# One one-hot matrix a batch instead of three, with shifted copies of keys and values: a two-layer cross-attention kernel

## The chip, the cores and the metric

The kernel runs on one core of one Trainium2 chip. The metric is the device time of one execution in microseconds (us). In the profile PE is the matrix engine (PEld its weight loads), DVE the vector engine, ACT the scalar engine, POOL the GpSimd engine, and SP the engine whose queue issues most of the DMA transfers.

## The reference, cut to what matters

There are 16 batches of 512 tokens by 256 features, and a context of 64 positions by 256 features for each batch. Two attention layers follow each other. The first has 16 heads of 16 features, and a token sees only the three context positions around its index:

```python
q = split(rmsnorm(x_tokens, gamma_q) @ Wq.T)      # 512 queries a batch, 16 heads of 16
k = split(kn @ Wk.T); v = split(kn @ Wv.T)        # 64 keys and values a batch
mask = abs(ctx_pos - ctx_index_per_token) <= 1    # positions index-1, index, index+1
w = where(mask, square(relu(q @ k.T / sqrt(hd))), 0)
out = (w / max(w.sum(-1), EPS_DEN)) @ v
x = x_tokens + out @ Wo.T
```

The second layer is a plain softmax attention over the 64 context positions with GELU on queries, keys and values, followed by a projection, a residual and a LayerNorm. Everything is float32; the kernel splits the operands of the large products into a high and a low part.

## The kernel before, in words

**Tiling.** A batch is one unit of work: 512 tokens by 256 features, held as two feature groups of 128 partitions. Keys and values of the first layer are computed once, at the start, for all batches, and stored in `kv0` as 128 rows: rows 0 to 63 hold the high parts of the 64 positions, rows 64 to 127 the low parts. Column group 0 is keys, column group 1 values.

**Picking by one-hot.** Instead of scoring all 64 positions, the kernel picks the three keys and the three values of each token by a matrix product with a one-hot matrix. For each shift `s` (0, 1, 2) DVE builds a 128x512 matrix that is 1 where the row's position, moved by `s - 1`, equals the token's index (`build_onehot`, L684). PE multiplies `kv0` by it: `picked_keys` (L386) gives keys 512 tokens wide, two products a shift; `picked_values` (L392) gives values 256 features wide, four products a shift. DVE multiplies picked keys with the queries (L697) and picked values with the normalised weights (`attend`, L738), and PE transposes and sums the results (`turn`, L411).

**Stages.** The 16 batches run as a software pipeline: step i handles the first half of layer one of batch i (`f`), the second half of batch i-1 (`b`), and the end of batch i-2 (`n`). Each engine has its own list of instructions, written by hand; an engine works strictly in the order of its list and waits at semaphores. At the end of step i, PE already picks the first keys of batch i+1 (`first_keys`).

**The start.** Before step 0 PE computes the keys and values of the context, eight tiles of two products (L324). ACT and DVE round and split them (L553, L670). SP moves them into `kv0` by 16 DMAs (L243, L244), eight for batches 0 to 7 and eight for batches 8 to 15; each group of eight waits for DVE (`prep_dve`). PE waits for the first eight of them (`kv0_in[0]`) before `first_keys(0)`. Behind the 16, SP's list has the loads of tokens and indices of batches 2 and 3 (L211, L212), the move of the second layer's values into `vfd` (L255), and then in each step the load for the batch three ahead.

**POOL** computes the low part of the tokens (L283), the reciprocal square roots, and the last scale and shift with the store of the output.

Of the kernel before, what the change touches and what calls it, by code (L numbers as in the profile page):

```python
# [19 lines left out]
C_ID, C_SEL, C_POS, C_EPS, C_END = 0, 128, 224, 227, 228  # L20


def xattn_pair(nc: bass.Bass, xT, ctx, ctxT, idx, vectors, wq0T, wk0T, wv0T, wo0T,
# [9 lines left out]
    with es:  # L33
# [10 lines left out]
        pos = [cst[:, C_POS + s:C_POS + s + 1] for s in range(SHIFTS)]  # L44
# [18 lines left out]
        onehot = sb("onehot", [P, SHIFTS, T], f32r)  # L63
# [4 lines left out]
        att = qkp[:, SHIFTS:2 * SHIFTS, :].rearrange("p s (j d) -> p s j d", j=TT)  # L68
# [4 lines left out]
        wn = sb("wn", [P, SHIFTS, TT, H])  # L73
# [16 lines left out]
        bufs = sb("bufs", [P, 8, DC * T])  # L90

        xsq, q0, xpT, q1T = (bufs[:, n, :].rearrange("p (c t) -> p c t", c=DC) for n in (0, 3, 4, 5))

        zn, zo = (bufs[:, n, :].rearrange("p (j d) -> p j d", j=TT) for n in (6, 7))
# [11 lines left out]
        v1T = bufs[:, 4:6, :]  # L106
        ctxT_sb = bufs[:, 6:8, :]
        vfn = rows(bufs[:, 6:8, :])
# [17 lines left out]
        kv0_in = [sem(f"kv0_in_{t}") for t in range(2)]  # L126
        prep_mm, prep_act, prep_dve, kvh_cp, vf_mm, vf_copied, vfd_in = map(sem, (
# [77 lines left out]
        def _(sp):  # L205
# [47 lines left out]
            for half in range(2):  # L253
                for odd in range(2):
                    sp.dma_start(vfd[half * K:(half + 1) * K, odd::2, :], vfn[odd * K:(odd + 1) * K, :, :]).then_inc(vfd_in, 16)  # L255
            for read in range(1, B - RING + 1):
# [5 lines left out]
                load(read + (RING - 1))  # L262
            for h in range(2):
# [50 lines left out]
        def _(pe):  # L314
# [68 lines left out]
            def picked_keys(f, s, bank0):  # L383

                for g in range(DC):
                    i = mm(ps[:, bank0 + g, :], kv0[:, f, 0, g * P:(g + 1) * P].bitcast(f32r), onehot[:, s, :], start=True, stop=True)  # L386
                i.then_inc(kg_mm, 1)

            def picked_values(f, s, bank0):

                for j in range(TT):
                    i = mm(ps[:, bank0 + j // 2, (j % 2) * D:(j % 2 + 1) * D], onehot[:, s, j * P:(j + 1) * P],  # L392
# [13 lines left out]
            def turn(f, s):  # L406

                pe.wait_ge(att_ready, 3 * f + s + 1)
                for g in range(DC):
                    for j in range(TT):  # L410
                        i = mm(ps[:, g, j * P:(j + 1) * P], att[:, s, j, g * P:(g + 1) * P], ident,  # L411
                               is_transpose=True, start=(s == 0 and j == 0), stop=(s == SHIFTS - 1), skip_group_check=True)
                    if s == SHIFTS - 1:
# [11 lines left out]
            def step(f, b, n, last=False):  # L425
# [62 lines left out]
                if f is not None:  # L488
# [5 lines left out]
                    picked_values(f, 0, 6)  # L494
# [154 lines left out]
        def _(dve):  # L649
# [28 lines left out]
            def build_onehot(f, shifts):  # L678
# [6 lines left out]
                if s == SHIFTS - 1:  # L685
                    i.then_inc(onehot_ready, 1)
# [162 lines left out]
```

## Time and profile before

| | |
|---|---|
| median of 3 runs | 422.99 us (420.45 to 423.73) |
| profiled execution, its own time | 423.02 us |
| its span in the trace | 421.2 us |
| PE busy | 384.7 us, 91% |
| DVE busy | 300.5 us, 71% |
| ACT busy | 222.4 us, 53% |
| POOL busy | 143.7 us, 34% |
| DMA engines, q1 (SP's queue) | 24.11 MB, 20.0% of 16 engines' span |

A share of busy time is an average over the whole span. The page also cuts the span into 40 slices and gives the busy share of each; the first four to six slices, the start, look different from the rest, which repeats with the period of a step. The time that lies outside the span is 423.02 less 421.2, which is 1.8 us. A time in the text is counted from the span's start.

### The profile page before, as it was taken

The numbers are of one execution on the slowest core, as the hardware profiler recorded it, in microseconds if no ns is written. First come the engines' busy times: TensorE is split into PE (matmuls) and PEld (weight loads), VectorE is DVE, ScalarE is ACT, GpSimd is POOL, SyncE is SP. The second block draws the span as 40 slices with busy tenths as digits, with TensorE's granted clock in tenths as the row PEclk, the third lists the DMA queues.
The fourth block names the chain that finished last, engine by engine and source line by source line (L and its number), as shares of the span: only waits on it lengthen the run. The fifth ranks groups of instructions, "written<-read, shape, count | busy, mean of one in ns | idle before, by whom it ended". The sixth has DMA issues, their size and how long they took to land.

```text
span 421.2 us, 5934 instructions
## 1 busy us (share of the span) xinstructions
PE 384.7 (91%) x2256; PEld 285.3 (68%) x2256; DVE 300.5 (71%) x592; ACT 222.4 (53%) x369; POOL 143.7 (34%) x100
## 2 busy tenths in 40 slices
PE   4799798999999999999999999999999999998770
PEld 1258666686868686868686868686868777776550
DVE  0334459587979797878787887878787879697614
ACT  0754412356556564646464656565656474737441
POOL 0102202023535353535353535353535353415151
PEclk9999999999999999999999999999999999999985
DMA  8901985802121212121212112020202101010111
GB/s 238 321 38 43 219 213 158 193 2 75 51 75 52 75 51 75 51 75 51 75 53 72 54 55 71 30 95 15 93 26 82 42 0 52 0 51 0 50 51 50
DMA packets 20333, 32.35 MB, mean 77 GB/s; under 512 B 1489, under 2 KB 11729, under 8 KB 20305
## 3 DMA queue, kind: packets, MB, share of 16 engines
q1 hardware_dynamic: 18144, 24.11, 20.0%
q0 software_dynamic: 2160, 7.87, 5.3%
q8 instruction: 18, 0.29, 0.3%
q14 instruction: 11, 0.08, 0.1%
HBM read 17.29 MB, written 8.39 MB: 61 GB/s over the span
## 4 chain that ended last, share of the span: by engine, by line
PE 78%; ACT 6%; issue 4%; DVE 4%; DMA 3%; SPq 2%; POOL 2%; ACTq 0%; DVEq 0%; POOLq 0%
PE ps L373 11%; PE ps L375 10%; PE ps L374 10%; PE ps L411 9%; PE ps L509 7%; PE ps L465 7%; PE ps L386 7%; PE ps L392 5%; PE ps L441 4%; PE ps L324 4%; PE ps L516 3%; ACT bufs L629 2%; DMA cst<-consts 2%; PE ps L478 2%; DMA kv<-qkp 1%
## 5 line engine op out<-in xcount | busy, mean ns | idle before, releaser
L283 POOL TENSOR_TENSOR x_lo<-x_ring,x_hi 128x1024 fp32r<-128x1024 f32 x16 | 38.1, 2380 | 124.9 <-ACT x_hi L568 124.9
L585 ACT ACTIVATE bufs<-ps,nbias,rstd 128x256 f32<-128x256 f32 x64 | 32.4, 563 | 65.5 <-issue 55.5
L303 POOL TENSOR_TENSOR bufs<-bufs,lng_row 128x1024 f32<-128x1024 f32 x15 | 35.9, 2394 | 84.5 <-ACT bufs L585 84.5
L738 DVE TENSOR_TENSOR qkp<-ps,wn 128x1024 f32<-128x1024 f32 x48 | 57.3, 1221 | 5.9 <-PE ps L392 4.5
L697 DVE TENSOR_TENSOR qkp<-ps,bufs 128x1024 f32<-128x1024 f32 x48 | 57.1, 1218 | 5.2 <-PE ps L386 5.2
L411 PE MATMUL ps<-cst,qkp 128*128 128x128 f32 x384 | 44.8, 273 | 0.0
L411 PEld LDWEIGHTS ps<-cst,qkp 128*128 128x128 f32 x384 | 42.6, 143 | 0.1
L386 PE MATMUL ps<-onehot,kv 128*128 128x512 f32 x96 | 34.4, 440 | 4.7 <-DMA kv<-qkp 2.1
L509 PE MATMUL ps<-k1T,bufs 128*128 128x64 f32 x256 | 32.0, 278 | 5.4 <-ACT bufs L629 5.4
L305 POOL TENSOR_TENSOR bufs<-bufs,lnb_row 128x1024 f32<-128x1024 f32 x15 | 35.5, 2366 | 1.2
L509 PEld LDWEIGHTS ps<-k1T,bufs 128*128 128x128 f32 x256 | 29.8, 191 | 8.9 <-ACT bufs L629 8.9
L392 PEld LDWEIGHTS ps<-kv,onehot 128*128 128x128 f32 x192 | 27.1, 189 | 10.0 <-ACT bufs L585 5.3
L392 PE MATMUL ps<-kv,onehot 128*128 128x256 f32 x192 | 33.3, 299 | 0.3 <-DVE wn L760 0.2
L465 PE MATMUL ps<-qkp,cst 128*32 128x512 f32 x192 | 30.7, 598 | 0.5 <-DVE qkp L697 0.5
L465 PE MATMUL ps<-bufs,cst 128*32 128x512 f32 x64 | 30.5, 598 | 0.0
L751 DVE TENSOR_REDUCE den<-ps 128x64 f32<-128x192 f32 x16 | 5.7, 358 | 34.3 <-ACT ps L620 34.3
L294 POOL TENSOR_TENSOR rstd<-var,minus_half 128x4 f32<-128x4 f32 x16 | 16.5, 1031 | 38.3 <-DVE var L720 38.3
L373 PE MATMUL ps<-xp_hi,wh_q 128*128 128x512 f32 x64 | 26.5, 414 | 2.3 <-DVE xp_lo L732 2.3
L732 DVE TENSOR_TENSOR xp_lo<-bufs,xp_hi 128x512 fp32r<-128x512 f32 x32 | 20.8, 688 | 10.3 <-ACT xp_hi L601 10.1
L640 ACT ACTIVATE o_hi<-ps 128x512 fp32r<-128x512 f32 x32 | 17.4, 595 | 19.9 <-PE ps L411 19.9
L373 PE MATMUL ps<-x_hi,wh_q 128*128 128x512 f32 x64 | 27.0, 422 | 0.0
L629 ACT ACTIVATE bufs<-ps,vec 128x512 f32<-128x512 f32 x32 | 22.0, 688 | 9.3 <-PE ps L375 9.1
(96 smaller groups left out, 820.8 us busy)
## 6 DMA issues: line engine op xcount, KB each, us to landing
x_ring<-xT SPq DMA_DIRECT2D x16, 512.0 KB, 3.6
out<-bufs POOLq DMA_DIRECT2D x15, 512.0 KB, 3.4
idx_ring<-idx SPq DMA_DIRECT2D x16, 256.0 KB, 4.2
kv<-qkp SPq DMA_DIRECT2D x8, 256.0 KB, 4.9
vfd<-bufs SPq DMA_DIRECT2D x4, 512.0 KB, 7.9
bufs<-ctxT SPq DMA_DIRECT2D x2, 512.0 KB, 6.5
qkp<-ctx SPq DMA_DIRECT2D x1, 1024.0 KB, 7.3
kv<-xp_hi SPq DMA_DIRECT2D x2, 256.0 KB, 4.1
```

Of the source, the lines that this page charges most:

```text
L283: G.tensor_tensor(x_lo[:, :, :], x_ring[:, f % RING, :, :], f32_view(x_hi[:, :, :]), ALU.subtract).then_inc(xl_ready, 2)
L303: G.tensor_tensor(zo, zn, lng_row[:, :].unsqueeze(1).broadcast_to([P, TT, D]), ALU.mult).then_inc(zg_ready, 1)
L373: mm(o, hi, m_hi, start=start, stop=False)
L374: mm(o, lo, m_hi, start=False, stop=False)
L375: last = mm(o, hi, m_lo, start=False, stop=stop)
L386: i = mm(ps[:, bank0 + g, :], kv0[:, f, 0, g * P:(g + 1) * P].bitcast(f32r), onehot[:, s, :], start=True, stop=True)
L392: i = mm(ps[:, bank0 + j // 2, (j % 2) * D:(j % 2 + 1) * D], onehot[:, s, j * P:(j + 1) * P], kv0[:, f, 1, :].bitcast(f32r), start=True, s ...
L411: i = mm(ps[:, g, j * P:(j + 1) * P], att[:, s, j, g * P:(g + 1) * P], ident, is_transpose=True, start=(s == 0 and j == 0), stop=(s == SHI ...
L465: i = mm(ps[32 * s:32 * s + 32, 4, :], sum_sel[:, g if s < SHIFTS else 2, :], qk[:, s, g, :] if s < SHIFTS else xsq[:, g, :], start=(g == ...
L509: i = mm(ps[:, 3, j * K:(j + 1) * K], q1T[:, c, j * P:(j + 1) * P], k1T[:, c, bass.ds(b * K, K)], start=(c == 0), stop=(c == DC - 1))
L697: V.tensor_tensor(qk[:, s, :, :], ps[:, bank0:bank0 + 2, :], q0, ALU.mult).then_inc(qk_ready, 1)
L738: V.tensor_tensor(att[:, s, :, :].rearrange("p j (h d) -> p (j h) d", d=HD), ps[:, bank0:bank0 + 2, :].rearrange("p a (h d) -> p (a h) d", ...
```

## The change

**One one-hot matrix.** A batch has a single one-hot matrix now, for the token's own position; the shifts 0 and 2 of the mask are no longer matrices. There are two buffers of it, used in turn, so that the matrix of the next batch is built while the present one is read.

**Shifted copies.** For the neighbours the keys and values themselves are moved: `kvs` holds, for each of two buffers, a copy of the batch's rows moved one row up (for index+1) and one moved one row down (for index-1). The copies are DMAs from `kv0`, issued by SP, four a batch, each 63 rows of 2 KB; the rows that no copy fills are zero from a memset of POOL at the start (`kvs_zero`). `first_keys` waits for the copies of its batch (`kvs_in`). The copies of batches 0 and 1 stand in SP's list behind the 16 DMAs into `kv0`; those of batch i+1 stand in step i behind the loads of tokens and indices.

**Order of the picks.** Keys are picked in the order index+1, index-1, centre. Values of both neighbours are picked in one product 512 wide for each of the four token tiles (`picked_neighbours`, two products a call, two calls), and the centre in four products 256 wide (`picked_centre`). `attend` has three calls of 1024 elements a partition as before, the layouts of `att` and `wn` are reordered to match, and `turn` has 8 transposes a call as before.

```diff
-        pos = [cst[:, C_POS + s:C_POS + s + 1] for s in range(SHIFTS)]
+        pos = cst[:, C_POS:C_POS + 1]
-        onehot = sb("onehot", [P, SHIFTS, T], f32r)
+        onehot = sb("onehot", [P, 2, T], f32r)
-        wn = sb("wn", [P, SHIFTS, TT, H])
+        wn = sb("wn", [P, TT, SHIFTS, H])
+        kvs_all = sb("kvs", [P, 2, 2, 2, D])
...
         @block.sync
+            def shifted(i):
+                r = i % 2
+                for lo in (0, K):
+                    sp.dma_start(kvs[lo:lo + K - 1, r, 0, :, :], kv0[lo + 1:lo + K, i, :, :]).then_inc(kvs_in[r], 16)
+                    sp.dma_start(kvs[lo + 1:lo + K, r, 1, :, :], kv0[lo:lo + K - 1, i, :, :]).then_inc(kvs_in[r], 16)
+            sp.wait_ge(kvs_zero, 1)
+            sp.wait_ge(kv0_in[0], 16 * 8)
+            shifted(0)
+            shifted(1)
             for i in range(2, RING):
...
+            def next_shifted(i):
+                if i == 8:
+                    sp.wait_ge(kv0_in[1], 16 * 8)
+                sp.wait_ge(kvs_in[i % 2], 64 * (i // 2))
+                sp.wait_ge(vg_mm, 3 * (i - 1))
+                shifted(i)
             for read in range(1, B - RING + 1):
...
                 load(read + (RING - 1))
+                next_shifted(read + 1)
+            for i in range(B - RING + 2, B):
+                next_shifted(i)
...
         @block.gpsimd
+            G.memset(kvs, 0.0).then_inc(kvs_zero, 1)
...
         @block.tensor
             def first_keys(f):
                 pe.wait_ge(onehot_ready, f + 1)
+                pe.wait_ge(kvs_in[f % 2], 64 * (f // 2 + 1))
                 picked_keys(f, 0, 4)
+            def picked_neighbours(f, pair, bank0):
+                for a in range(2):
+                    j = 2 * pair + a
+                    i = mm(ps[:, bank0 + a, :], onehot[:, f % 2, j * P:(j + 1) * P],
+                           kvs[:, f % 2, :, 1, :].bitcast(f32r),
+                           start=True, stop=True)
+                i.then_inc(vg_mm, 1)
...
-                    picked_values(f, 0, 6)
+                    picked_neighbours(f, 0, 6)
                     pe.wait_ge(wn_ready, f + 1)
-                    picked_values(f, 1, 4)
+                    picked_neighbours(f, 1, 4)
-                    picked_values(f, 2, 6)
+                    picked_centre(f, 6)
...
         @block.vector
+            def build_onehot(f):
                 dve.wait_ge(idx_in, 16 * f + 16)
-                if not first(f):
-                    dve.wait_ge(vg_mm, 3 * f)
-                for s in shifts:
-                    i = V.tensor_scalar(onehot[:, s, :], idx_ring[:, f % RING, :], pos[s], None, ALU.is_equal)
+                if f > 1:
+                    dve.wait_ge(vg_mm, 3 * (f - 1))
+                V.tensor_scalar(onehot[:, f % 2, :], idx_ring[:, f % RING, :], pos, None, ALU.is_equal).then_inc(onehot_ready, 1)
...
                 if f is not None:
+                    if not last:
+                        build_onehot(f + 1)
                     dve.wait_ge(w_ready, f + 1)
...
-                    if not last:
-                        build_onehot(f + 1, range(0, 2))
...
-                if f is not None and not last:
-                    build_onehot(f + 1, range(2, SHIFTS))
```

**SP at the start, before.** These are the rows of SP's list from the last two DMAs into `kv0` on (`kv`), with the loads of batches 2 and 3 behind them.

```order
L243 DMA kv<-o_lo 64x4x256
L244 DMA kv<-qkp 64x4x256
L211 DMA x_ring<-xT 128x2x512 [waits idx_in,x_in]
L212 DMA idx_ring<-idx 128x512
L211 DMA x_ring<-xT 128x2x512 [waits idx_in,x_in]
```

**SP at the start, in the change.** The same place, where `kvs` is the tensor of the shifted copies.

```order
L248 DMA kv<-o_lo 64x4x256
L249 DMA kv<-qkp 64x4x256
L254 DMA kvs<-kv 63x512 [waits kv0_in_0,kvs_zero]
L255 DMA kvs<-kv 63x512
L254 DMA kvs<-kv 63x512
L255 DMA kvs<-kv 63x512
L254 DMA kvs<-kv 63x512
L255 DMA kvs<-kv 63x512
L254 DMA kvs<-kv 63x512
L255 DMA kvs<-kv 63x512
L216 DMA x_ring<-xT 128x2x512 [waits idx_in,x_in]
L217 DMA idx_ring<-idx 128x512
```

Eight copies, four for batch 0 and four for batch 1, stand behind all 16 DMAs into `kv0` and ahead of the loads.

**DVE in step 1, before.** These are DVE's rows from the end of `head` to the low part of the layer's output; L684 builds a one-hot matrix.

```order
L732 TENSOR_TENSOR xp_lo<-bufs,xp_hi 128x512 [waits xph_ready] x2
L751 TENSOR_REDUCE den<-ps 128x64 [waits w_ready]
L754 TENSOR_TENSOR dcl<-den,ps 128x64 [waits den_ready]
L758 RECIPROCAL rden<-dcl 128x64 [waits dcl_ready]
L760 TENSOR_TENSOR wn<-ps,rden 128x192 [waits rden_ready]
L738 TENSOR_TENSOR qkp<-ps,wn 128x1024 [waits vg_mm,o_mm,wn_ready]
L738 TENSOR_TENSOR qkp<-ps,wn 128x1024 [waits vg_mm] x2
L684 TENSOR_SCALAR onehot<-idx_ring,cst 128x512 [waits vg_mm,idx_in]
L684 TENSOR_SCALAR onehot<-idx_ring,cst 128x512
L779 TENSOR_REDUCE smax<-ps 128x4 [waits sc_mm]
L781 TENSOR_TENSOR sdiff<-ps,smax 128x256 [waits smax_ready]
L684 TENSOR_SCALAR onehot<-idx_ring,cst 128x512 [waits vg_mm,idx_in]
```

**DVE in step 1, in the change.** The same place.

```order
L772 TENSOR_TENSOR xp_lo<-bufs,xp_hi 128x512 [waits xph_ready] x2
L726 TENSOR_SCALAR onehot<-idx_ring,cst 128x512 [waits vg_mm,idx_in]
L800 TENSOR_REDUCE den<-ps 128x64 [waits w_ready]
L803 TENSOR_TENSOR dcl<-den,ps 128x64 [waits den_ready]
L807 RECIPROCAL rden<-dcl 128x64 [waits dcl_ready]
L809 TENSOR_TENSOR wn<-ps,rden 128x192 [waits rden_ready]
L785 TENSOR_TENSOR qkp<-ps,wn 128x2x512 [waits vg_mm,o_mm,wn_ready]
L785 TENSOR_TENSOR qkp<-ps,wn 128x2x512 [waits vg_mm]
L785 TENSOR_TENSOR qkp<-ps,wn 128x4x256 [waits vg_mm]
L826 TENSOR_REDUCE smax<-ps 128x4 [waits sc_mm]
```

One build is left, and it stands ahead of the reduction of the weights (`den`) instead of behind the multiplications with the values.

**PE in step 1, in the change.** These rows take the place of L392 x4, L392 (waits wn_ready), L392 x3, the six products of the second layer's queries, and L392 x4.

```order
L422 MATMUL ps<-kvs,onehot 128x512 x2
L422 MATMUL ps<-kvs,onehot 128x512 [waits wn_ready]
L422 MATMUL ps<-kvs,onehot 128x512
L401 MATMUL ps<-xp_hi,wh_q 128x512
L402 MATMUL ps<-xp_hi,wl_q 128x512
L403 MATMUL ps<-xp_lo,wh_q 128x512
L401 MATMUL ps<-xp_hi,wh_q 128x512
L402 MATMUL ps<-xp_hi,wl_q 128x512
L403 MATMUL ps<-xp_lo,wh_q 128x512
L430 MATMUL ps<-kv,onehot 128x256 [waits att_ready]
```

Eight products 256 wide became four 512 wide; their waits stand where they stood.

## Rows read from the trace of the kernel before

**Rows 1.** The page: PE's busy tenths in 40 slices; the chain that ended last.

```profile
PE   4799798999999999999999999999999999998770
...
PE 78%; ACT 6%; issue 4%; DVE 4%; DMA 3%; SPq 2%; POOL 2%; ACTq 0%; DVEq 0%; POOLq 0%
```

**Rows 2.** Busy time by stretch (start:end, length, each engine), one whole step.

```profile
core 0: us, PE busy (x) PEld busy (x) DVE busy (x) ACT busy (x) POOL busy (x), PEclk, DMA share, GB/s
199.00:220.65 21.65, 21.28 (x134) 16.07 (x134) 17.58 (x35) 12.69 (x20) 9.20 (x6) 1.00 0.18 62
```

**Rows 3.** Timeline of SP (start, us to issue, line), DMAs into kv0 and the loads behind.

```profile
55.41 1.16 SPq L244 DMA_DIRECT2D kv<-qkp  x1
56.66 1.69 SPq L211 DMA_DIRECT2D x_ring<-xT  x1
```

**Rows 4.** Timeline of PE at the start of step 0 (idle before in brackets).

```profile
47.14 1.89 PE L367 MATMUL ps<-vfd,bufs 128*128 128x256 f32 x8
51.16 1.20 PE L386 MATMUL ps<-onehot,kv 128*128 128x512 f32 x4 [2.14 <-DMA kv<-qkp]
```

**Rows 5.** DMAs issued between 38 and 62 us: mean rate, and us to landing.

```profile
DMA packets 4680, 4.84 MB, mean 202 GB/s; under 512 B 273, under 2 KB 4369, under 8 KB 4679
...
kv<-qkp SPq DMA_DIRECT2D x8, 256.0 KB, 4.9
...
x_ring<-xT SPq DMA_DIRECT2D x1, 512.0 KB, 5.6
```

**Rows 6.** The page: DMA issues of the whole span, KB each, us to landing.

```profile
x_ring<-xT SPq DMA_DIRECT2D x16, 512.0 KB, 3.6
```

**Rows 7.** PE's first matmuls, groups of 5.9-11.5 us and 12.2-16 us (mean ns).

```profile
L324 PE MATMUL ps<-bufs,vfd 128*128 128x512 f32 x7 | 6.3, 1079 | 6.0 <-DMA bufs<-ctxT 6.0
L324 PE MATMUL ps<-bufs,vfd 128*128 128x512 f32 x10 | 4.9, 642 | 0.0
```

**Rows 8.** A stretch as in rows 2, after a wait of PE (PEclk: granted clock).

```profile
18.70:22.40 3.70, 3.70 (x5) 1.62 (x6) 2.85 (x10) 1.77 (x4) 0.00 (x0) 0.54 0.83 221
```

**Rows 9.** Waits by engine: us in total, times, longest.

```profile
POOL cmean L276 <- ACT x_ring L549: 15.8, 1, 15.8
...
PE ps L324 <- ACT k1T L553: 2.5, 1, 2.5
```

**Rows 10.** Timeline of DVE at the end of step 0.

```profile
67.75 1.27 DVE L684 TENSOR_SCALAR onehot<-idx_ring,cst 128x512 fp32r<-128x512 int32 x3
68.94 1.28 DVE L794 TENSOR_TENSOR o_lo<-ps,o_hi 128x512 fp32r<-128x512 f32 x2
```

**Rows 11.** Timeline of PE in a later step, around the picks of values.

```profile
211.09 0.40 PE L375 MATMUL ps<-xp_lo,wh_q 128*128 128x512 f32 x1
211.42 1.44 PE L392 MATMUL ps<-kv,onehot 128*128 128x256 f32 x8
212.70 0.40 PE L373 MATMUL ps<-xp_hi,wh_q 128*128 128x512 f32 x1
...
213.86 0.39 PE L375 MATMUL ps<-xp_lo,wh_q 128*128 128x512 f32 x1
214.09 0.63 PE L392 MATMUL ps<-kv,onehot 128*128 128x256 f32 x4
215.03 0.32 PE L509 MATMUL ps<-k1T,bufs 128*128 128x64 f32 x1 [0.31 <-ACT bufs L629]
```

**Rows 12.** Timeline of DVE in the same step.

```profile
210.47 0.36 DVE L751 TENSOR_REDUCE den<-ps 128x64 f32<-128x192 f32 x1 [2.00 <-ACT ps L620]
...
215.90 1.07 DVE L684 TENSOR_SCALAR onehot<-idx_ring,cst 128x512 fp32r<-128x512 int32 x2
217.06 0.42 DVE L779 TENSOR_REDUCE smax<-ps 128x4 f32<-128x256 f32 x1
```

**Rows 13.** Timeline of SP in the same step.

```profile
206.48 0.38 SPq L211 DMA_DIRECT2D x_ring<-xT  x1
```

**Rows 14.** Timeline of PE at the end of that step.

```profile
220.50 1.48 PE L386 MATMUL ps<-onehot,kv 128*128 128x512 f32 x4
```

More of the change, by code:

```diff
@@ L89, in xattn_pair @@
         nbias = sb("nbias", [P, TT])
-        bufs = sb("bufs", [P, 8, DC * T])
-        xsq, q0, xpT, q1T = (bufs[:, n, :].rearrange("p (c t) -> p c t", c=DC) for n in (0, 3, 4, 5))
-        zn, zo = (bufs[:, n, :].rearrange("p (j d) -> p j d", j=TT) for n in (6, 7))
+        kvs_all = sb("kvs", [P, 2, 2, 2, D])
+        kvs = kvs_all[:, :, :, :, :]
+        bufs = sb("bufs", [P, 7, DC * T])
+        xsq, q0, xpT, q1T = (bufs[:, n, :].rearrange("p (c t) -> p c t", c=DC) for n in (0, 2, 3, 4))
+        zn, zo = (bufs[:, n, :].rearrange("p (j d) -> p j d", j=TT) for n in (5, 6))
         def rows(t):
@@ L105, in xattn_pair @@
         kv_lo = [[rows(qkp[:, n:n + 1, :]) for n in pair] for pair in ((0, 4), (1, 5))]
[L106 to L108 removed]
+        v1T = bufs[:, 3:5, :]
+        ctxT_sb = bufs[:, 5:7, :]
+        vfn = rows(bufs[:, 5:7, :])
         raw = {n: vfd[:, 2 * i:2 * i + 2, :] for i, n in enumerate(("k0", "v0", "k1", "v1", "f1", "q0", "o0", "q1"))}
@@ L126, in xattn_pair @@
         kv0_in = [sem(f"kv0_in_{t}") for t in range(2)]
+        kvs_zero = sem("kvs_zero")
+        kvs_in = [sem(f"kvs_in_{r}") for r in range(2)]
         prep_mm, prep_act, prep_dve, kvh_cp, vf_mm, vf_copied, vfd_in = map(sem, (
@@ L385, in picked_keys, with picked_centre @@
                 for g in range(DC):
-                    i = mm(ps[:, bank0 + g, :], kv0[:, f, 0, g * P:(g + 1) * P].bitcast(f32r), onehot[:, s, :], start=True, stop=True)
+                    keys = kv0[:, f, 0, :] if s == CENTRE else kvs[:, f % 2, s, 0, :]
+                    i = mm(ps[:, bank0 + g, :], keys[:, g * P:(g + 1) * P].bitcast(f32r), onehot[:, f % 2, :], start=True, stop=True)
                 i.then_inc(kg_mm, 1)
-            def picked_values(f, s, bank0):
+            def picked_neighbours(f, pair, bank0):
[5 more added lines that the diff above has]
+                i.then_inc(vg_mm, 1)
+            def picked_centre(f, bank0):
                 for j in range(TT):
-                    i = mm(ps[:, bank0 + j // 2, (j % 2) * D:(j % 2 + 1) * D], onehot[:, s, j * P:(j + 1) * P],
+                    i = mm(ps[:, bank0 + j // 2, (j % 2) * D:(j % 2 + 1) * D], onehot[:, f % 2, j * P:(j + 1) * P],
                            kv0[:, f, 1, :].bitcast(f32r),
@@ L404, in queries0, with turn @@
                     product(ps[:, e, :], *weight("q0", c, e), x_hi[:, c, :], x_lo[:, c, :], c == 0, c == DC - 1, q0_mm)
-            def turn(f, s):
-                pe.wait_ge(att_ready, 3 * f + s + 1)
+            def turn(f, part):
+                pe.wait_ge(att_ready, 3 * f + part + 1)
+                if part < CENTRE:
+                    tiles = [(2 * part + a, s) for a in range(2) for s in range(2)]
+                else:
+                    tiles = [(j, CENTRE) for j in range(TT)]
                 for g in range(DC):
[L410 to L413, printed above, removed]
+                    for j, s in tiles:
+                        i = mm(ps[:, g, j * P:(j + 1) * P], att[:, j, s, g * P:(g + 1) * P], ident,
+                               is_transpose=True, start=(j == 0 and s == 0), stop=(s == CENTRE), skip_group_check=True)
+                    if part == CENTRE:
                         i.then_inc(o_mm, 1)
@@ L734, in tail, with attend @@
             def tail(f, b, last=False):
-                def attend(s, bank0):
-                    dve.wait_ge(vg_mm, 3 * f + s + 1)
-                    V.tensor_tensor(att[:, s, :, :].rearrange("p j (h d) -> p (j h) d", d=HD),
-                                    ps[:, bank0:bank0 + 2, :].rearrange("p a (h d) -> p (a h) d", d=HD),
-                                    wn[:, s, :, :].rearrange("p j h -> p (j h)").unsqueeze(2).broadcast_to([P, TT * H, HD]),
+                def attend(part, bank0):
+                    dve.wait_ge(vg_mm, 3 * f + part + 1)
+                    if part < CENTRE:
+                        rows, shifts = slice(2 * part, 2 * part + 2), slice(0, 2)
+                    else:
+                        rows, shifts = slice(0, TT), slice(CENTRE, SHIFTS)
+                    out_to = att[:, rows, shifts, :].rearrange("p j s d -> p j (s d)").rearrange("p j (h d) -> p j h d", d=HD)
+                    groups = wn[:, rows, shifts, :].rearrange("p j s h -> p j (s h)")
+                    n_j, n_g = groups.shape[1], groups.shape[2]
+                    V.tensor_tensor(out_to,
+                                    ps[:, bank0:bank0 + 2, :].rearrange("p a n -> p (a n)").rearrange("p (j h d) -> p j h d", j=n_j, d=HD),
+                                    groups.unsqueeze(3).broadcast_to([P, n_j, n_g, HD]),
                                     ALU.mult).then_inc(att_ready, 1)
@@ L817, in shape_constants @@
     c[:, C_SEL + 64] = 16.0 * EPS_DEN / D
-    for s in range(SHIFTS):
-        c[:, C_POS + s] = r % K - 1 + s
+    c[:, C_POS] = r % K
     c[96, C_EPS] = 16.0 * EPS_DEN * EPS_RMS
```

14 lines of the change are left out of this document (6 added, 8 removed).

## The prediction

> **What bounds the kernel now.** I read the page first, then one whole step, then the start, then the few microseconds around each edit. PE's busy tenths are nines from the fifth slice on, and PE's instructions make up 78% of the chain that ended last [rows 1]. In one whole step PE is busy 21.28 of 21.65 us, DVE 17.58, ACT 12.69 [rows 2]. So in the steady part a gain must shorten PE's own list or one of its few waits; work saved on DVE counts only where PE waits for DVE. The start is another regime: PE's slices there are not full [rows 1], and what PE waits for is a DMA. It ends its last product of the preparation and then idles 2.14 us until the first eight DMAs into `kv0` have landed; at 51.16 us it picks the first keys [rows 4].
>
> **The start: the copies for batch 0.** This is the term that decides. PE's first keys now also wait for the shifted copies of batch 0. SP issues in the order of its list, and there the copies stand behind all 16 DMAs into `kv0`, not behind the eight they depend on. The last of the 16 is issued from 55.41 to 56.57 us, and SP's next instruction began at 56.66 [rows 3]. So the first copy can be issued at 56.66 at the earliest, 5.5 us after PE used to start. The condition for the early half is long met then, so the delay is the queue's and not the data's.
>
> How long from there until the four copies of batch 0 have landed? The trace has no copy of 63 rows, so I bound it.
> - From below: issues like the later token load, 0.38 us each [rows 13], put the fourth issue at 56.66 + 3 x 0.38 = 57.8, and 3.6 us from issue to landing, the median of the token loads, most of them in an empty queue [rows 6], gives 61.4.
> - From above: 1.69 us an issue, as the token load behind the full queue took [rows 3], puts the fourth issue at 61.7, and 5.6 us to landing as that load took [rows 5] gives 67.3.
> - By bytes: the last DMA into `kv0` lands about 55.41 + 4.9 = 60.3 [rows 3, 5]. Behind it are 4 x 63 x 2 KB = 0.516 MB at the measured 202 GB/s [rows 5], 2.6 us. That gives 62.9.
>
> I take 62.9, since these DMAs are limited by what the engines move (256 KB each at an issue of 1.2 us is the same rate of about 215 GB/s). PE's first keys come at 62.9 and not at 51.16: **+11.7 us**, bounds +10.2 and +16.1. Nothing covers it: the rest of PE's step 0 is in the list behind `first_keys`, and the loads of batches 2 and 3, which the copies also push back by some 4 us, are needed only in steps 1 and 2.
>
> **The start: PE's clock.** PE then idles from about 49.0 to 62.9. The trace shows what follows a wait. The kernel's first 128x512 products take 1079 ns, those from 12.2 us on 642 ns [rows 7], so after its first idle stretch PE ran low for some 6 us, from 5.9 to about 12. After another wait of 2.5 us for ACT [rows 9], the stretch from 18.7 to 22.4 us has a granted clock of 0.54, which is the 1.2 GHz level for nearly all of it [rows 8]. PE at half clock for 3.7 to 6.2 us does half the work of that time and so loses 1.8 to 3.1 us; the work behind `first_keys(0)` is nearly unbroken PE work. I take **+2.3 us**. The Trainium skill (TensorE: Matmul & The Clock Gate, section Part 1: The HAM clock gate) says that the array's clock is throttled by default and that activity releases it; the rows agree, and by it the step 0 after a wait this long would start low, as I have assumed.
>
> **The end of step 0.** Before, DVE built three matrices in 1.27 us [rows 10] between its last product and `o_lo`, and PE waited for both. Now the next matrix is built earlier, in the wait for ACT. But ACT's `o_hi` comes only about 0.4 us before `o_lo` began, so `o_lo` moves forward by that, and PE's third keys with it: **-0.4 us**, bounds 0 and -1.3.
>
> **PE's picks in each step.** Eight products 256 wide become four 512 wide. Row L392 x8 starts at 211.42 and the next product at 212.70 [rows 11]; of these 1.28 us about 0.1 is a wait for `wn`, so a 256-wide product takes its turn every (1.28 - 0.1) / 8 = 0.15 at most. The four without a wait last 0.63 with the last one's own 0.28, so 0.35 / 3 = 0.12 apart. A 512-wide one takes 214.09 - 213.86 = 0.23 [rows 11]. Two narrow ones cost 0.24, one wide one 0.23: 4 x 0.01 x 16 = **-0.5 us** at most, with a floor of 0. The mean of 299 ns that the page gives for such a product is its latency, which overlaps with the next one and is not what PE pays. The fewer weight loads cost nothing before, since they run beside the products.
>
> **DVE's two matrices fewer.** L684 x2 takes 1.07 us, so DVE saves 1.07 us in each of 15 steps [rows 12]. I cost it at nothing. The two builds stand at 215.90, and the next work, `smax`, starts at 217.06 when PE's scores, begun at 215.03 [rows 11], are complete; the cover is PE's own work, and without the builds DVE waits. The remaining build, about 0.5 us, moves in front of `den`, where DVE idles 2.00 us for ACT [rows 12]. If ACT were 1.5 us earlier this would delay `wn` and PE; it is not. The multiplications with the values have as many elements as before and 1.07 us of new slack behind them.
>
> **The copies in each later step.** SP issues the token load at 206.48 [rows 13] and the index load, then four copies: 206.48 + 6 x 0.5 = about 209.5 for the last issue, and 5.6 us to landing [rows 5] gives 215.1. PE needs them at 220.50 [rows 14], 5.4 us later. SP's new waits are for things long done, and nothing but the next step's loads is queued behind them. So: nothing. The memset on POOL lies in the 15.8 us that POOL waits for ACT [rows 9].
>
> **Sum.** 11.7 + 2.3 - 0.4 - 0.5 = +13.1 us on the profiled execution's own 423.0, which is 436.1; that execution is at the median of the runs shown (422.99), so nothing is to be corrected. The bounds add up to 10.2 + 1.8 - 1.3 - 0.5 = +10.2 and 16.1 + 3.1 = +19.2; they will hardly all fall on one side.
>
> **Rivals.**
> - Narrow copies. 63 rows do not divide over 16 DMA engines as 64 or 128 do, and each copy runs on part of them. On half of the engines the 0.516 MB take 5.1 us and not 2.6: +2.5, so 438.6. In later steps the 5.4 us of slack still cover it. No row of before has such a shape, for or against; I give it 0.25. The Trainium skill (DMA: Bandwidth & Descriptors, section Why a DMA increments its semaphore by 16 and not by 1) says that a transfer runs on the largest number of engines up to 16 that divides its slowest dimension, which is 9 here, and this speaks against copies of 63 rows; by it the rate would be 9/16 of 202 GB/s and the sum 438.1. No run of before shows it.
> - The steady step gets shorter by what DVE saves: if PE waited for DVE somewhere in each step, 15 x 1.07 = 16 us would come off, and 436.1 becomes 420.1, below the time of before. It decides from 0.9 us a step on (13.1 / 15). Against it: PE is idle only 0.37 us in a step [rows 2], and the wait that it names is for ACT, 0.31 us [rows 11]. Chance 0.05.
> - The copies come late in every step: they need more than 14 us from SP's issue at 206.48 to landing [rows 13, 14]. Four copies on one or two DMA engines, 0.516 MB at 202/16 or 202/8 GB/s, take 41 or 20 us. Then each of 14 steps is longer by at least 6 us: over 520 us. Chance 0.03.
> - The reordered layout makes `wn` slower. PE waits for `wn` already, so each ns counts. Were it to take as long again as the reduction of the same 192 elements beside it, 0.36 us [rows 12], 15 x 0.36 = 5.4 us: 441.5. Chance 0.07.
> - The start hides more than I see, as with copies that land at 61.4 and a clock that recovers at once: 436.1 - 1.5 - 2.3 = 432.3. I count this to the forecast; the low end leaves 1.8 us below it for copies that, being a quarter of a token load, land sooner than one.
>
> **Numbers.** The forecast has 0.60, the narrow copies 0.25, slower `wn` 0.07, DVE's saving 0.05, late copies 0.03. A range of 430.5 to 441.5 takes in the forecast's bounds on both sides, the narrow copies and most of the slower `wn`; I put 0.82 in it. A measurement of this kernel can tell about 1%, or 4.2 us, from no change. Faster by over that: 0.03; within it: 0.05, from the rival of DVE's saving; slower: 0.92.
>
> **What would show it.** In the new profile SP issues the first copy at about 56.7 and PE's first keys wait for a DMA into `kvs` and start at about 63. After that the granted clock is low for some microseconds. The steps keep a period of about 21.6 us, DVE's wait before `smax` grows by about 1 us, and PE never waits for `kvs` after step 0. I would be wrong if SP issued the copies before 56 us, if PE's first keys came before 60 or after 68, or if the period moved by more than 0.2 us.

## The result and the profile after

The changed kernel takes 437.65 us (median of 4 runs, 436.07 to 439.06), the kernel before 423.36 us in the runs beside it. The ratio is 1.034, with a 95% interval of 1.026 to 1.042: slower by 14.3 us, where 13.1 us were forecast. The profiled execution has a span of 434.8 us against 421.2.

The page of the changed kernel answers to [rows 1]: busy time by engine, then PE's busy tenths and granted clock in 40 slices, then the chain that ended last.

```profile
PE 385.1 (89%) x2192; PEld 281.0 (65%) x2192; DVE 285.5 (66%) x560; ACT 222.2 (51%) x369; POOL 145.3 (33%) x101
...
PE   4699609899999999999999999999999999998860
...
PEclk9889958999999999999999999999999999999995
...
PE 77%; ACT 6%; SPq 6%; issue 4%; DVE 3%; DMA 3%; POOL 2%; ACTq 0%; DVEq 0%; POOLq 0%
```

DVE has 15.0 us less to do (300.5 before), and none of it shows in the time. PE has as much to do as before, 64 instructions fewer included. The sixth slice of PE is a 0, and in the chain SP's queue has 6% where it had 2. One whole step by stretch, against [rows 2]:

```profile
220.70:242.30 21.60, 21.24 (x130) 15.73 (x129) 16.61 (x33) 12.68 (x22) 9.18 (x6) 1.00 0.24 85
```

The steady part is what it was: PE fills 21.24 of 21.60 us. The loss is at the start. SP's timeline (start, us to issue, line), against [rows 3]:

```profile
39.76 0.73 SPq L248 DMA_DIRECT2D kv<-xp_hi  x1
...
56.63 1.21 SPq L249 DMA_DIRECT2D kv<-qkp  x1
57.94 1.58 SPq L254 DMA_DIRECT2D kvs<-kv  x1
59.56 1.19 SPq L255 DMA_DIRECT2D kvs<-kv  x1
60.80 0.70 SPq L254 DMA_DIRECT2D kvs<-kv  x1
61.54 0.70 SPq L255 DMA_DIRECT2D kvs<-kv  x1
```

And PE's, against [rows 4]:

```profile
48.34 1.89 PE L395 MATMUL ps<-vfd,bufs 128*128 128x256 f32 x8
64.90 2.04 PE L415 MATMUL ps<-onehot,kvs 128*128 128x512 f32 x4 [14.67 <-DMA kvs<-kv]
66.74 2.85 PE L395 MATMUL ps<-vfd,bufs 128*128 128x256 f32 x8
```

The first copy is issued 0.1 us after the last of the 16 DMAs into `kv0`, and PE waits 14.67 us for the copies where it waited 2.14 for `kv0`. Behind the wait the same eight products of L395 take 2.85 us, where they took 1.89. A stretch right behind the wait and the next one, with the columns of [rows 2], show why:

```profile
64.90:68.70 3.80, 3.80 (x9) 3.06 (x10) 2.36 (x2) 0.00 (x0) 0.00 (x0) 0.50 0.68 201
68.70:72.00 3.30, 3.30 (x20) 2.23 (x23) 1.91 (x4) 0.00 (x0) 0.00 (x0) 1.00 0.32 123
```

The granted clock is 0.50 for the first 3.8 us, the 1.2 GHz level.

### The profile page after: what moved, and what is told of

Same layout as the page of the kernel before. It is cut to its first block, busy times and chain, and to the rows that moved or that the text cites. A ratio compares the mean times of both kernels' runs of the same rounds, so it can differ in the third digit from the quotient of the medians.

```text
span 434.8 us, 5852 instructions
## 1 busy us (share of the span) xinstructions
PE 385.1 (89%) x2192; PEld 281.0 (65%) x2192; DVE 285.5 (66%) x560; ACT 222.2 (51%) x369; POOL 145.3 (33%) x101
## 4 chain that ended last, share of the span: by engine, by line
PE 77%; ACT 6%; SPq 6%; issue 4%; DVE 3%; DMA 3%; POOL 2%; ACTq 0%; DVEq 0%; POOLq 0%
PE ps L401 10%; PE ps L454 9%; PE ps L403 9%; PE ps L402 9%; PE ps L552 7%; PE ps L415 6%; PE ps L508 6%; PE ps L422 5%; PE ps L352 4%; PE ps L484 4%; PE ps L559 3%; ACT bufs L672 2%; SPq L249 2%; DMA cst<-consts 2%; SPq L248 2%
## 5 line engine op out<-in xcount | busy, mean ns | idle before, releaser
L415 PE MATMUL ps<-onehot,kvs 128*128 128x512 f32 x64 | 23.3, 449 | 16.7 <-DMA kvs<-kv 14.7
L352 PE MATMUL ps<-bufs,vfd 128*128 128x512 f32 x32 | 19.2, 767 | 9.5 <-DMA bufs<-ctxT 6.0
L659 ACT ACTIVATE s_sb<-ps,cst 128x512 f32<-128x512 f32 x16 | 11.0, 687 | 29.7 <-PE ps L508 29.7
L403 PE MATMUL ps<-xp_lo,wh_q 128*128 128x512 f32 x64 | 25.3, 396 | 0.0
```

The source lines that it names most:

```text
L352: last = mm(ps[:, 4 + n % 4, 0:cols], stationary, moving, start=(i == 0), stop=(i == len(parts) - 1))
L403: last = mm(o, hi, m_lo, start=False, stop=stop)
L415: i = mm(ps[:, bank0 + g, :], keys[:, g * P:(g + 1) * P].bitcast(f32r), onehot[:, f % 2, :], start=True, stop=True)
```

## The experiments

Each is the changed kernel with one edit, except e9 and e10, which are the two kernels once more. A ratio is to the kernel before in the runs beside it: 423.36 us beside the change, 422.27 beside e1, e2, e3 and e5, 423.43 beside e4, e6, e7 and e8. So the medians of two experiments, most of them of four runs that spread over 1 to 3 us, tell little below 2 us. Where an effect is smaller, it is read from stretches of the traces.

**e2_no_copy0: the start without the copies of batch 0.**

```diff
-            shifted(0)
...
-                pe.wait_ge(kvs_in[f % 2], 64 * (f // 2 + 1))
+                if f:
+                    pe.wait_ge(kvs_in[f % 2], 64 * (f // 2 + f % 2))
+                else:
+                    pe.wait_ge(kvs_zero, 1)
```

> The changed kernel without the four copies of batch 0 and without PE's wait for them; the neighbours of batch 0 are left out of the computation (their rows stay zero), all else is as in the change. My theory is that the whole loss is the start: PE's first keys come when the first eight DMAs into kv0 have landed, about 14.7 - 2.1 = 12.5 us earlier than in the change, and PE's clock does not fall (1.6 us). Then the time is 437.65 - 12.5 - 1.6 = about 423, the level of the kernel before less what the steady part saves (0.7 us), 422 to 424. Rival: the copies or the new layouts cost in every step; then most of the 14 us stays and the time is over 432.

Measured: 422.34 us against 422.27 of before, ratio 0.9995 (0.9963 to 1.0027). The whole loss is gone, the wait and the low clock behind it together. PE's first keys are back at the landing of the first eight DMAs into `kv0`:

```profile
51.12 1.19 PE L415 MATMUL ps<-onehot,kvs 128*128 128x512 f32 x4 [2.24 <-DMA kv<-qkp]
52.16 1.89 PE L395 MATMUL ps<-vfd,bufs 128*128 128x256 f32 x8
```

What follows: the copies, the layouts and the wide picks of all later batches cost nothing together within the interval of 0.3%, which is 1.3 us; nor do they gain anything that this measurement tells.

**e1_copies_ahead: the copies of batch 0 between the two groups of eight DMAs.**

```diff
             for t in range(2):
+                if t == 1:
+                    sp.wait_ge(kvs_zero, 1)
+                    sp.wait_ge(kv0_in[0], 16 * 8)
+                    shifted(0)
                 sp.wait_ge(prep_dve, 2 * 4 * (t + 1))
...
-            shifted(0)
             shifted(1)
```

> The changed kernel with the four copies of batch 0 moved in SP's list between the first eight and the second eight DMAs into kv0, so that they no longer queue behind the second eight; the copies of batch 1 stay behind those. If the place in SP's queue is the cause, the first copy is issued when the first eight have landed (about 51 to 52 us), the last about 2.2 us later, and with 3.3 us to landing PE's first keys start at 56.5 to 57.5 and not at 64.9: 8 us less, 429 to 430, with PE's clock still low after the wait. The rival, that the copies are slow in themselves (63 rows on a part of the DMA engines), expects less: first keys after 60 us and 433 or more.

Measured: 428.65 us, ratio 1.014 (1.009 to 1.018). SP and PE in its timelines:

```profile
46.20 1.34 SPq L260 DMA_DIRECT2D kv<-qkp  x1
50.86 0.88 SPq L246 DMA_DIRECT2D kvs<-kv  x1
51.79 0.75 SPq L247 DMA_DIRECT2D kvs<-kv  x1
52.59 0.70 SPq L246 DMA_DIRECT2D kvs<-kv  x1
53.33 0.70 SPq L247 DMA_DIRECT2D kvs<-kv  x1
```

```profile
56.66 2.04 PE L417 MATMUL ps<-onehot,kvs 128*128 128x512 f32 x4 [7.56 <-DMA kvs<-kv]
```

The first keys come at 56.66, inside the 56.5 to 57.5 expected; the time is just below the 429 to 430 expected. By the ratios 7.9 us of the loss are gone by moving four DMAs in a list, and the two spans (434.8 and 426.9) differ by as much. What is left of it is the chain that the data need: the first eight land, then four copies are issued and land, 50.86 to 56.66.

**e3_rows64: 64 rows in a copy and not 63.**

```diff
-                    sp.dma_start(kvs[lo:lo + K - 1, r, 0, :, :], kv0[lo + 1:lo + K, i, :, :]).then_inc(kvs_in[r], 16)
-                    sp.dma_start(kvs[lo + 1:lo + K, r, 1, :, :], kv0[lo:lo + K - 1, i, :, :]).then_inc(kvs_in[r], 16)
+                    sp.dma_start(kvs[lo:lo + K, r, 0, :, :], kv0[lo:lo + K, i, :, :]).then_inc(kvs_in[r], 16)
+                    sp.dma_start(kvs[lo:lo + K, r, 1, :, :], kv0[lo:lo + K, i, :, :]).then_inc(kvs_in[r], 16)
```

> The changed kernel with copies of 64 rows at the same place instead of 63 rows moved by one (the shift is left out of the computation: both neighbours are the centre). Four copies are then 0.524 MB and not 0.516 MB. If 63 rows run on a part of the DMA engines, 64 rows land sooner: in the trace of the change 2 KB packets moved at about 160 GB/s while the eight copies ran, and here they should move at over 250 GB/s, PE's first keys come about 1.5 us earlier than at 64.9, and SP's issue of a copy takes less than 0.70 us in the steady part. The time is 435.5 to 436.5. The rival that the shape does not matter expects the same 64.9 and 437.65 within noise.

Measured: 435.08 us, ratio 1.030 (1.025 to 1.036), 2.6 us below the change and 1.5 us by the ratios; 435.5 to 436.5 were expected. The profiled execution is the slowest of the four (437.39), so only stretches of it are compared. SP's first copy is at 56.96 and PE's first keys at 62.77:

```profile
56.96 1.43 SPq L254 DMA_DIRECT2D kvs<-kv  x1
58.43 1.19 SPq L255 DMA_DIRECT2D kvs<-kv  x1
59.66 0.60 SPq L254 DMA_DIRECT2D kvs<-kv  x1
```

```profile
62.77 2.04 PE L415 MATMUL ps<-onehot,kvs 128*128 128x512 f32 x4 [13.60 <-DMA kvs<-kv]
```

That is 5.8 us from the first copy's issue to the keys, where the change needs 64.90 - 57.94 = 7.0 (7.1 in e10, its second trace: 56.87 to 64.00), so 63 rows cost 1.15 to 1.3 us. The last two columns of a stretch in which nearly all traffic was copies are the busy share of the 16 DMA engines and the rate; first the change, then this kernel:

```profile
62.00:66.00 4.00, 1.10 (x3) 0.94 (x4) 0.00 (x0) 0.00 (x0) 0.00 (x0) 0.50 0.49 158
```

```profile
60.50:64.50 4.00, 1.74 (x4) 1.48 (x5) 0.44 (x1) 0.00 (x0) 0.00 (x0) 0.50 0.88 208
```

With 63 rows the engines are busy 49% and move 158 GB/s, with 64 rows 88% and 208. In the second stretch a token load is issued at 63.58; before it, from 61.0 to 63.5 us, it is 86% and 202. So copies of 63 rows leave about half of the engines' time idle. The share is a mean over 16 engines and does not tell whether some of them get nothing. The rate is not the 250 GB/s that I expected of 64 rows: in the second stretch a busy engine moves less (158 / 0.49 = 322 GB/s at full share against 208 / 0.88 = 236). The issue is 0.60 us and not 0.70. The edit changes two things, the number of rows and the shift by one row. That the number counts, e7 (below) shows: its four extra copies have 63 rows and no shift, take 2.99 us to issue, 0.75 each, and from 225.5 to 227.5 us the engines are busy 52% at 173 GB/s.

**e5_filler: PE kept busy in the wait.**

```diff
+            for _ in range(60):
+                mm(ps[:, 2, :], w_hi["q0"][:, 0, 0:P], w_hi["q0"][:, :, :].rearrange("p c d -> p (c d)"), start=True, stop=True)
             pe.wait_ge(kv0_in[0], 16 * 8)
             first_keys(0)
```

> The changed kernel with 60 extra products of 128x512 on PE between its last product of the preparation and the wait for the copies, into a bank of the accumulator that nobody reads before it is overwritten; they take 60 x 0.23 = 13.8 us of the 14.7 us that PE idles. If the low clock after the wait costs what I read from the trace (3.8 us at the 1.2 GHz level from 64.9 on), the granted clock stays at 1.00, the stretch from the first keys to the end of step 0's last product is 1.6 us shorter, and the time is 436. The rival, that the low clock is covered by other waits in step 0, expects no change in that stretch.

Measured: 435.93 us, ratio 1.031 (1.025 to 1.038). That is 1.7 us below the change, but 0.6 by the ratios, and its runs (434.24 to 437.70) overlap those of the change: the total does not show the 1.6 us. The timeline of PE does:

```profile
48.91 13.98 PE L466 MATMUL ps<-wh_q 128*128 128x512 f32 x60
63.91 1.16 PE L415 MATMUL ps<-onehot,kvs 128*128 128x512 f32 x4 [1.01 <-DMA kvs<-kv]
64.90 1.89 PE L395 MATMUL ps<-vfd,bufs 128*128 128x256 f32 x8
...
68.77 0.63 PE L510 MATMUL ps<-qkp,cst 128*32 128x512 f32 x3
```

Behind the wait the granted clock is 1.00, where it was 0.50 in the change:

```profile
64.00:68.00 4.00, 4.00 (x18) 3.13 (x19) 3.06 (x3) 0.00 (x0) 0.00 (x0) 1.00 0.80 228
```

The eight products take 1.89 us again, and from the first keys to the head sums (L510 here) it is 4.9 us, as before (51.16 to 56.07); in the change it is 64.90 to 71.37, 6.5 us. The low clock costs 1.6 us there. The work is the same, and only what PE did during the wait differs. The span is only 0.4 us shorter than in the change (434.4), though PE was 2.6 us ahead at the first product with `o_hi` (84.28 against 86.91): behind the start of the last products with `k1T` this execution took 35.6 us to the end and that of the change 33.5; the section on the prediction shows how this end varies.

**e4_narrow_picks: the neighbours picked 256 wide.**

```diff
-                    i = mm(ps[:, bank0 + a, :], onehot[:, f % 2, j * P:(j + 1) * P],
-                           kvs[:, f % 2, :, 1, :].bitcast(f32r),
-                           start=True, stop=True)
+                    for s in range(2):
+                        i = mm(ps[:, bank0 + a, s * D:(s + 1) * D], onehot[:, f % 2, j * P:(j + 1) * P],
+                               kvs[:, f % 2, s, 1, :].bitcast(f32r),
+                               start=True, stop=True)
```

> The changed kernel with the values of the neighbours picked 256 wide: eight products for four. By the rows of before and after, a 256-wide product takes its turn every 0.12 us and a 512-wide one every 0.23, so a step is longer by 4 x 0.01 = 0.04 us, back from 21.60 to about 21.64 to 21.66, and the time is 438.3 at most. The rival, that the wide products save what the page's means say (299 ns for a narrow one, about 400 for a wide one, so 0.8 us a step), expects 450.

Measured: 438.16 us against 437.65, a difference within the spread of either. The picks and the product behind them, first in the change, then here:

```profile
226.00 1.43 PE L422 MATMUL ps<-kvs,onehot 128*128 128x512 f32 x4
227.27 0.39 PE L401 MATMUL ps<-xp_hi,wh_q 128*128 128x512 f32 x1
```

```profile
227.47 1.45 PE L423 MATMUL ps<-kvs,onehot 128*128 128x256 f32 x8
228.75 0.39 PE L401 MATMUL ps<-xp_hi,wh_q 128*128 128x512 f32 x1
```

Four wide products take their turn in 1.27 us and eight narrow ones in 1.28. The wide pick is worth 0.01 us a step. Twelve steps, counted as under e9 below, are 21.61 us each here and 21.60 in the change, a little less than the 21.64 to 21.66 expected. The rival that goes by the profile page's mean durations has fallen.

**e8_builds_back: DVE's saving given back.**

```diff
                     if first(f):
                         copy_final_values(range(6, CT))
+                    if not last:
+                        for s in range(2):
+                            V.tensor_scalar(extra[:, s, :], idx_ring[:, (f + 1) % RING, :], pos, None, ALU.is_equal)
```

> The changed kernel with two more matrices built by DVE in each step at their old place behind the multiplications with the values, into a buffer that nobody reads. DVE is busy 1.07 us longer in each of 15 steps. By my theory this is taken from DVE's wait before smax, the period stays 21.60 us and the time 437.65. The rival, that DVE's saving counts in the step and was given back elsewhere, expects up to 16 us more.

Measured: 438.15 us, 0.5 us above the change, within the spread; twelve steps are 21.61 us each. DVE in the change, then here:

```profile
226.88 3.68 DVE L785 TENSOR_TENSOR qkp<-ps,wn 128x1024 f32<-128x1024 f32 x3 [0.23 <-PE ps L422]
231.63 0.42 DVE L826 TENSOR_REDUCE smax<-ps 128x4 f32<-128x256 f32 x1 [1.07 <-PE ps L552]
```

```profile
230.75 1.07 DVE L826 TENSOR_SCALAR extra<-idx_ring,cst 128x512 fp32r<-128x512 int32 x2
231.91 0.42 DVE L830 TENSOR_REDUCE smax<-ps 128x4 f32<-128x256 f32 x1
```

The saving of 1.07 us a step is exactly the idle time that DVE has in front of `smax`, and putting the work back fills it. Only the step from the 14th to the 15th is 0.4 us longer here than in the change (20.86 against 20.48), which stays unexplained.

**e7_more_copies: twice the copies in each step.**

```diff
                 sp.wait_ge(vg_mm, 3 * (i - 1))
+                if i > 2:
+                    sp.wait_ge(kvx_in, 64 * (i - 2))
+                for lo in (0, K):
+                    for s in range(2):
+                        sp.dma_start(kvx[lo:lo + K - 1, i % 2, s, :, :], kv0[lo:lo + K - 1, i, :, :]).then_inc(kvx_in, 16)
                 shifted(i)
```

> The changed kernel with four more copies in each step ahead of the four that count, into a buffer that nobody reads: eight copies of 63 rows a step. In the trace of the change a step's copies are issued by 225.1 us, and PE needs them at 235.1. The extra four put them off by 4 x 0.75 = 3 us, so they land at about 231 to 232, still in time: the period stays 21.60 us and the time 437.65. The rival, that the steps' copies are near the edge or disturb the engines by their traffic, expects a longer period.

Measured: 436.82 us against 437.65, no difference that can be told, and steps of 21.61 us. The last copy that counts is issued at 227.51, 3.1 us later than in the change, and PE's only wait for `kvs` is that of step 0.

**e9_before_again and e10_after_again: second traces.**

> The kernel before once more, for a second trace. Its first trace has steps of 21.62 to 21.66 us (mean 21.65), all kernels with the change 21.60 to 21.615. If the step is really shorter in the change, this trace has 21.65 again; the rival, that it differs from one execution to the next by 0.05 us, expects a mean of 21.60 to 21.62 here. SP's first DMA into kv0 came at 38.57 in the first trace of before and at 39.76 in that of the change; if that is the length of PE's low clock after 18.7 us, it moves with that length here too and has nothing to do with the change.

> The changed kernel once more. If the 1.2 us by which the preparation ended later in the first trace come from the length of the low clock alone, then with the shorter low stretch SP's first DMA into kv0 is issued at about 38.6 and PE's first keys at 63.8, and with the longer one at 39.8 and 64.9 again. The rival is that the memset of POOL or another part of the change slows the preparation: then it is 39.8 with the shorter low stretch too.

Measured: 421.94 us (e9) and 438.93 us (e10), one run each. The chain of waits gives the start of the products with `k1T` (the first value is the start in us) 12 steps apart, in the first trace of before, in this one of before, and in the change:

```profile
106.75 2.00 PE ps L509 x16
...
366.52 2.00 PE ps L509 x16
```

```profile
107.17 2.00 PE ps L509 x16
...
366.53 2.00 PE ps L509 x16
```

```profile
121.59 2.00 PE ps L552 x16
...
380.79 2.00 PE ps L552 x16
```

The steps are 21.65, 21.61 and 21.60 us long. So the shorter step that the first pair of traces shows differs from one execution of before to the next by most of its size, and I do not count it as a gain of the change. As to the start, e10 issued its first DMA into `kv0` at 38.56 us, as before (38.57), and its PE began the first keys at 64.00:

```profile
64.00 2.04 PE L415 MATMUL ps<-onehot,kvs 128*128 128x512 f32 x4 [14.96 <-DMA kvs<-kv]
```

The 1.2 us by which the preparation ended later in the first trace of the change are thus not the change's. The rival with the memset has fallen.

**e6_direct: the copies of batch 0 past SP's queue.** POOL issues them from the tensors in which ACT and DVE write the first tile's high and low parts.

```diff
+            pool.wait_ge(kvs_zero, 1)
+            pool.wait_ge(prep_dve, 2)
+            for m in range(2):
+                for dst, rows_of in ((0, f32_view(kv_hi[m][0][0:K, 0, :])), (K, kv_lo[m][0][0:K, 0, :])):
+                    pool.dma_start(kvs[dst:dst + K - 1, 0, 0, m, :], rows_of[1:K, :]).then_inc(kvs_first, 16)
+                    pool.dma_start(kvs[dst + 1:dst + K, 0, 1, m, :], rows_of[0:K - 1, :]).then_inc(kvs_first, 16)
...
-            shifted(0)
...
-                pe.wait_ge(kvs_in[f % 2], 64 * (f // 2 + 1))
+                if f:
+                    pe.wait_ge(kvs_in[f % 2], 64 * (f // 2 + f % 2))
+                else:
+                    pe.wait_ge(kvs_first, 16 * 8)
...
-            pe.wait_ge(kv0_in[0], 16 * 8)
             first_keys(0)
...
+                    if first(f):
+                        pe.wait_ge(kv0_in[0], 16 * 8)
                     picked_keys(f, 2, 4)
...
+                    if first(f):
+                        dve.wait_ge(kv0_in[0], 16 * 8)
+                        dve.wait_ge(kvs_first, 16 * 8)
```

> The changed kernel with the copies of batch 0 taken from where ACT and DVE write the keys and values (before SP moves them into kv0), issued by POOL as soon as the first tile is ready, eight copies of 63 rows of 1 KB. They no longer queue behind SP's 16 DMAs. PE's first keys need nothing of kv0 then and start behind the last product of the preparation at about 49 us; DVE's first multiplication waits for the first eight DMAs into kv0 (about 51.1 us), since it overwrites what they read. By my theory this takes away the whole start cost and about 1.2 us more: PE's third keys at about 52.5 us and not at 53.7 as in the kernel before. The time is 421 to 422, between the same and 0.6% faster than the kernel before. The rival, that POOL's copies land late because they share the DMA engines with SP's or that POOL is too slow to issue them, expects first keys after 52 us and 424 or more.

Measured: 422.67 us over 12 runs, against 423.43 of before over 17; ratio 0.997 (0.9941 to 0.9999). PE in its timeline:

```profile
49.10 1.89 PE L403 MATMUL ps<-vfd,bufs 128*128 128x256 f32 x8
50.64 1.28 PE L423 MATMUL ps<-onehot,kvs 128*128 128x512 f32 x4
...
54.50 0.73 PE L423 MATMUL ps<-onehot,kv 128*128 128x512 f32 x2 [0.86 <-DVE qkp L752]
```

PE goes from its last product of the preparation into the first keys with no wait. Its preparation ended 1.9 us later than in the trace of before (SP's first DMA at 40.50), and taken from there the third keys come after 14.0 us and not after 15.2 (53.74 less 38.57). This version beats the changed kernel by 3.4%. Against the kernel before it is 0.3% faster, and the interval ends at 0.9999: the start cost is gone, but a gain over the kernel before is hardly told from none. The time expected, 421 to 422, was about a microsecond too low; of the 1.2 us at the third keys DVE, which now sets the next product by its second multiplication, gives back 0.5.

## Why the prediction was right, point by point

**The copies behind 16 DMAs** (forecast +11.7 us). Right in mechanism and nearly in size. From SP's first DMA into `kv0` to PE's first keys it is 12.6 us before (38.57 to 51.16), 25.1 in the change (39.76 to 64.90) and 25.4 in its second trace: +12.6 and +12.9. e2 shows that the whole loss, this wait and the low clock behind it, comes from the copies of batch 0. e1 shows that the place in SP's list is 7.1 us of the wait: the first keys come 18.05 us behind the first DMA into `kv0` (38.61 to 56.66) and not 25.1. The issue of the first copy was foreseen at 0.1 us behind the last DMA, and it came so. The term measures 12.6 us, 0.9 more than forecast. The mis-sized step is the landing: I moved the 0.516 MB at the 202 GB/s of DMAs of 64 rows, and they moved at 158, so they took 3.3 us and not 2.6.

**Narrow copies** (a rival with 0.25 at +2.5). Its mechanism is there too, at about half the price: 1.15 us by e3, 1.3 with the second trace. With 64 rows the keys come 62.77 - 38.67 = 24.1 us behind the first DMA, +11.5, which is the forecast term. So the likeliest case and this rival both held; I should have given the rival more than a quarter, since nothing in the trace spoke against it and the Trainium skill (DMA: Bandwidth & Descriptors, section Why a DMA increments its semaphore by 16 and not by 1) spoke for it. By its rule 9 of 16 engines work, 56% of them; the traces agree, with 49% busy against 88% with 64 rows, which is 0.56 of it. The sum by that rule, 438.1, is the nearest to the measured time, but partly by luck: it prices the narrow copies at 2.0 us, and they cost 1.15 to 1.3.

**The low clock** (+2.3, bounds +1.8 and +3.1). It cost 1.6 us in the trace of the change, where 3.8 us behind the wait were low; e5 takes it away. That is 0.7 us less than forecast and below my lower bound. In e10 the clock was low for 5.8 us behind the same wait, which cost 2.6 us by the same stretch (64.00 to 71.48), and once more in step 1:

```profile
64.00:69.80 5.80, 5.79 (x14) 4.60 (x15) 2.36 (x2) 0.00 (x0) 0.00 (x0) 0.50 0.65 197
...
86.90:90.30 3.40, 3.40 (x10) 2.62 (x9) 2.19 (x3) 0.00 (x0) 0.97 (x1) 0.50 0.97 218
```

That execution took 438.93 us. The term is a range, and my value lies between the two measured ones. The second drop the prediction did not have at all: the products with `o_hi` up to the next queries take 4.3 us and not 2.7, so it costs 1.6 us. Two of the four runs of the change have the mean clock of e10, 0.959, and took 438.66 and 439.06 us; the other two have 0.964 and 0.967 and took 436.65 and 436.07. So the median of the change likely has a part of this drop in it. Its cause stays open: from 83.4 to 86.9 us PE was busy 1.96 us in e10 and 1.97 in the change, which has no drop. A long wait for copies is not needed for one, since the trace of e6 has a granted clock of 0.53 from 73.0 to 76.6 us.

**The end of step 0** (-0.4). From the start of the transposes of step 0 to the first product with `o_hi` it is 6.54 us before (65.44 to 71.98) and 6.16 after (80.75 to 86.91): -0.38. No experiment isolates it.

**The picks** (-0.5 at most). 0.01 us a step by e4, so 0.2 in all, below what can be told.

**DVE's two matrices fewer** (nothing), **the copies in later steps** (nothing), **the memset** (nothing). Shown by e8, by e7, and by e10. SP needs 0.70 us to issue a copy, not the 0.5 that I took, which the slack covers.

**The rivals that fell.** DVE's saving counts (e8), late copies in every step (e7), slower `wn`: DVE's row for it is 0.36 us in both kernels, and e2's time leaves no room for it.

**The sum.** The terms as measured, 12.6 + 1.6 - 0.4, make 13.8 us, and the same three make 13.6 in the forecast. That they agree so well is luck in part: 0.9 us too little for the copies and 0.7 too much for the clock nearly cancel. The spans differ by 13.6, and that this is so near to 13.8 is luck too: beside the terms the preparation ended 1.2 us later, and step 1 (0.1), the 12 steps behind it (0.6) and the end (0.7) were shorter by 1.4 us in all. The end is not the change's. From the start of the last products with `k1T` to the end of the span it is 34.2 us in the first trace of before, 33.1 in its second and 33.5 in the change. Most of what differs is one row of the chain, in front of POOL's last reciprocal root; first before, then e9:

```profile
406.60 6.72 issue
```

```profile
406.60 5.65 issue
```

It is 6.08 us in the change and 8.19 in e5. The granted clock of that stretch is 0.61, 0.95 and 0.73 in before, e9 and the change, so the longer it is, the lower the clock. The 0.04 us a step between the first trace of before and the others stay open.

The upper end of my range does not fit my bounds: 423.0 + 19.2 is 442.2, and the range ends at 441.5, so it did not take in the bounds on both sides, as I wrote.

## What to carry to other kernels

Ask of each new DMA not only what it depends on but what stands ahead of it in the list of the engine that issues it: here the data had landed at 51 us and the queue came to them at 57, and the first work of a pipeline has no earlier step to hide in. Work taken from an engine that waits for another, and fewer but wider products on an engine that moves the same columns, are worth nothing until the trace shows someone waiting for them. A wait of PE as long as this one (14.67 us) costs more than its length, since the work behind it starts at half clock: 1.6 us more here.

## What was not expected of the hardware

The length of the low clock varies from run to run, and the spread of this kernel's times goes with it: of the 17 runs of before beside e6 the fastest, 420.81 us, has a mean granted clock of 0.985 and the slowest, 426.81, one of 0.972. A clock lower by 0.013 over 421 us is 5.5 us of full clock, and the two times are 6.0 apart. After PE's 2.5 us wait at the start the clock came back within 3.7 us in the first trace of before, but in that of e6 the stretch behind is still mostly low; first before, then e6:

```profile
22.40:26.00 3.60, 3.60 (x9) 1.52 (x8) 2.44 (x5) 1.37 (x3) 0.00 (x0) 1.00 0.05 20
```

```profile
22.40:26.00 3.60, 3.60 (x6) 1.43 (x6) 2.27 (x5) 0.69 (x1) 0.00 (x0) 0.60 0.00 2
```

The traces with the longer low stretch (the change, e6, e7, e8) issue the first DMA into `kv0` at 39.7 to 40.5 us, those with the shorter one (before and e9, e1 to e5, e10) at 38.4 to 39.0. That is up to 2 us in a total of 423, more than the gain of e6, and only many runs average it out.

A copy of 63 rows takes SP 0.70 us to issue even with an empty queue, and one of 64 rows 0.60, where a token load of 128 rows and four times the bytes takes 0.38.
